# Inverse rows of the last task loaded step by step, 46 rows a load instead of 48, and three pairs of banks for the held groups

## What is computed

```python
# layer 0                                      # layer 1
f  = fft2(x);  Xh = (f.real - f.imag)[:, :, :46]   xf = rfft2(x)                      # complex
o1 = relu(Xh @ w1[0] + b1[0])                      o1r, o1i = relu(complex product with w1, + b1)
o2 = o1 @ w2[0] + b2[0]                            o2r, o2i = softshrink(complex product with w2, + b2)
x  = ifft2(softshrink(o2)).real + x                x = irfft2(o2r + 1j*o2i) + x
```

## Time and profile before

| what | us |
|---|---|
| runs, median (low to high) | 519.73 (518.99 to 520.14) |
| the profiled execution, its own time | 518.5 |
| its span, first to last instruction | 516.7 |
| PE busy | 475.7 (92%) |
| DVE, ACT, POOL busy | 306.7, 209.5, 173.1 |
| bytes read from and written to HBM | 52.21 and 51.43 MB |

### The profile page before, as it was taken

The page is one execution under the profiler, slowest core; times in us unless marked ns, Lnnn a source line. Parts: engine busy times, 40 slices in busy tenths (PEclk is TensorE's granted clock), DMA queues, the critical chain, the costliest instruction groups (busy, mean ns, idle before and its releaser), DMA issues.

```text
span 516.7 us, 14864 instructions
## 1 busy us (share of the span) xinstructions
PE 475.7 (92%) x6144; PEld 341.0 (66%) x6144; DVE 306.7 (59%) x674; ACT 209.5 (41%) x473; POOL 173.1 (34%) x194
## 2 busy tenths in 40 slices
PE   3479999999999999999999999999999999998773
PEld 1157787767777677767777776767777777876531
DVE  6534455457754677457754677456764577567643
ACT  0025544643445443543354442554355433434201
POOL 9822313223341344223441244313442123222124
PEclk9859999999999999999999999999999999999967
DMA  8889763667989588977889688977989565644397
GB/s 182 264 229 258 198 192 91 148 204 193 261 230 238 158 229 245 231 207 186 256 238 219 173 198 256 234 201 182 261 222 256 158 176 158 145 100 129 114 257 226
DMA packets 76864, 104.63 MB, mean 203 GB/s; under 512 B 7777, under 2 KB 63319, under 8 KB 76798
## 3 DMA queue, kind: packets, MB, share of 16 engines
q1 hardware_dynamic: 57766, 56.74, 41.1%
q0 software_dynamic: 10608, 40.45, 29.5%
q10 hardware_dynamic: 8424, 6.49, 5.1%
HBM read 52.21 MB, written 51.43 MB: 201 GB/s over the span
## 4 chain that ended last, share of the span: by engine, by line
PE 79%; DVE 6%; DMA 6%; POOL 3%; ACT 2%; issue 2%; SPq 1%; ACTq 1%; POOLq 0%; DVEq 0%
PE ps L620 14%; PE ps L686 13%; PE ps L711 12%; PE ps L673 11%; PE ps L587 10%; PE ps L633 8%; PE ps L698 5%; PE ps L649 4%; PE ps L659 3%; DMA img<-x 2%; DVE img L566 2%; DVE ns L540 2%; POOL xs L384 2%; ACT p L457 1%; DVE nt L518 1%
## 5 line engine op out<-in xcount | busy, mean ns | idle before, releaser
L566 DVE TENSOR_TENSOR img<-ps,img 90x768 f32<-90x768 f32 x92 | 82.6, 900 | 20.3 <-PE ps L620 16.9
L384 POOL TENSOR_TENSOR xs<-xs,nt 128x360 f32<-128x360 f32 (+1 forms) x48 | 41.6, 866 | 147.9 <-DVE nt L518 120.6
L620 PE MATMUL ps<-jr,cst 64*90 64x384 f32 (+1 forms) x358 | 81.5, 525 | 6.7 <-DVE img L566 5.7
L587 PE MATMUL ps<-img,cst 128*64 128x384 f32 (+1 forms) x368 | 70.8, 500 | 9.7 <-DMA img<-x 9.7
L393 POOL DMA_DIRECT2D y<-img x42 | 34.8, 828 | 133.5 <-DVE img L566 133.2
L450 ACT ACTIVATE o<-ps,wt 97x180 f32<-97x180 f32 (+1 forms) x96 | 33.8, 406 | 107.6 <-PE ps L673 107.6
L633 PEld LDWEIGHTS ps<-cst,bt 128*64 128x64 f32 x1472 | 63.2, 141 | 20.4 <-issue 13.9
L540 DVE SCALAR_TENSOR_TENSOR ns<-p,ps 109x384 f32<-109x384 f32 x96 | 53.2, 554 | 37.8 <-ACT p L457 32.9
L633 PE MATMUL ps<-cst,bt 128*64 128x90 f32 x1472 | 69.0, 248 | 6.1 <-DMA bt<-scr_f 6.1
L686 PE MATMUL ps<-wt,o 128*64 128x96 f32 x1472 | 73.9, 249 | 0.2 <-DVE o L532 0.2
L686 PEld LDWEIGHTS ps<-wt,o 128*64 128x64 f32 x1472 | 64.9, 137 | 12.3 <-issue 12.3
(11 more groups left out here) (41 smaller groups left out, 403.0 us busy)
## 6 DMA issues: line engine op xcount, KB each, us to landing
y<-img POOLq DMA_DIRECT2D x35, 540.0 KB, 5.4
img<-x POOLq DMA_DIRECT2D x30, 540.0 KB, 8.3
scr_i<-et SPq DMA_DIRECT2D x48, 270.0 KB, 5.6
scr_f<-fs SPq DMA_DIRECT2D x154, 72.0 KB, 3.3
bt<-scr_f SPq DMA_DIRECT2D x40, 270.0 KB, 5.2
jr<-scr_i SPq DMA_DIRECT2D x48, 216.0 KB, 5.3
img<-x ACTq DMA_DIRECT2D x10, 540.0 KB, 6.9
y<-img SPq DMA_DIRECT2D x11, 270.0 KB, 3.5
```

The source lines that it names most:

```text
L384: nc.gpsimd.tensor_tensor(re, re, nt[s % 2][:, :, 0:kws(s), 0:H], ALU.subtract).then_inc(re_ok, 1)
L566: nc.vector.tensor_tensor(y, p, y, ALU.add).then_inc(i_add, 1)
L587: last = mm(ps[64 * r:64 * r + 64, P3 + g % 2, 0:(b - a) * HC], K["w_fwd"], img[t % IMGS][:, a:b, :].rearrange("p h c -> p (h c)"), start= ...
L620: last = mm(ps[0:W, B0 + r, 0:n], K["w_inv"][64 * r:64 * r + 64, :], set_rows(t, j)[64 * r:64 * r + 64, at, 0:n], start=True, stop=True)
```

## The change

Three things are edited. The loads and stores of `scr_i` take only the 23 frequencies in use (`kws(s)` of a step, `2 * KW` = 46 rows) instead of 24. The last task's inverse rows go to `f0` (the first task's buffer, long free), eight rows with each step, behind the next step's store, and the last six behind the last store, half from SyncE and half from ScalarE; `jr` and `bt` aren't used for them. The held groups rotate over the bank pairs P2, P1, P3; and three groups, not four, go through ScalarE and GpSimd, over two buffers (`p1` and an idle `et`), and are stored from ScalarE's queue.

```diff
+HELD = 7
-LAST_POOL = (1, 4, 7, 10)
+LAST_POOL = (1, 4, 7)
...
     order += held
-    order += [("rows", TASKS - 1, j) for j in range(len(JSETS))]
+    order.append(("last_rows",))
     order += [("inv", TASKS - 1, g) for g in range(GROUPS)]
...
+        def last_rows(i, r):
+            k0, k1 = 2 * STEP * i, min(2 * STEP * (i + 1), 2 * KW)
+            rows = scr_i[TASKS - 1].rearrange("k e h c -> (k e) h c")[k0:k1]
+            four = rows[:, 0:H - 1, :].rearrange("q (g r s) c -> q g r (s c)", r=2, s=2)[:, :, r, :]
+            return four, f0[64 * r + k0:64 * r + k1, 0:GROUPS - 1, :], rows[:, H - 1, :], f0[k0:k1, GROUPS - 1, 0:HC]
+        def held_no(t, g):
+            return g - HELD if t == TASKS - 2 else -1
+        def pair_of(t, g):
+            if t == TASKS - 1:
+                return (P0, P1, P2, P3)[g % 4]
+            return (P2, P1, P3)[held_no(t, g) % 3] if held_no(t, g) >= 0 else P3
...
 # SyncE, a step's store
-                    sp.dma_start(scr_i[t][STEP * i:STEP * i + STEP].rearrange("k e h c -> (e h) k c"),
-                                 et[s % 2][0:2 * H, :, :]).then_inc(e_st[s % 2], 16)
+                    sp.dma_start(scr_i[t][STEP * i:STEP * i + kws(s)].rearrange("k e h c -> (e h) k c"),
+                                 et[s % 2][0:2 * H, 0:kws(s), :]).then_inc(e_st[s % 2], 16)
+                    if t == TASKS - 1 and i > 0:
+                        sp.wait_ge(e_st[(s - 1) % 2], 16 * ((s - 1) // 2 + 1))
+                        for r in range(2):
+                            four, to, one, to_one = last_rows(i - 1, r)
+                            sp.dma_start(to, four).then_inc(l_ld[0], 16)
+                        sp.dma_start(to_one, one).then_inc(l_ld[0], 16)
...
 # SyncE, a set of inverse rows (all tasks but the last)
-                    rows = scr_i[t].rearrange("k e h c -> (k e) h c")
+                    rows = scr_i[t].rearrange("k e h c -> (k e) h c")[0:2 * KW]
                     if g0 == GROUPS - 1:
-                        sp.dma_start(set_rows(t, j)[0:2 * KWP, 0, 0:HC], rows[:, 4 * g0, :]).then_inc(landed, 16)
+                        sp.dma_start(jr[k][0:2 * KW, 0, 0:HC], rows[:, 4 * g0, :]).then_inc(j_ld[k], 16)
...
-                            sp.dma_start(set_rows(t, j)[64 * r:64 * r + 2 * KWP, 0:g1 - g0, :], four[:, :, r, :]).then_inc(landed, 16)
+                            sp.dma_start(jr[k][64 * r:64 * r + 2 * KW, 0:g1 - g0, :], four[:, :, r, :]).then_inc(j_ld[k], 16)
+                if kind == "last_rows":
+                    sp.wait_ge(e_st[(NT - 1) % 2], 16 * ((NT - 1) // 2 + 1))
+                    four, to, one, to_one = last_rows(STEPS - 1, 0)
+                    sp.dma_start(to, four).then_inc(l_ld[0], 16)
+                    sp.dma_start(to_one, one).then_inc(l_ld[0], 16)
...
 # ScalarE, the three groups for GpSimd
-                    nc.scalar.activation(p1[0:W], ps[0:W, B0:B0 + 2, 0:2 * HC], ACT.Copy).then_inc(i_act, 1)
+                    if n > 1:
+                        act.wait_ge(i_pool, n - 1)
+                    p = (p1[0:W], et[NT % 2][0:W].rearrange("p (r s) c -> p r (s c)", r=2))[n % 2]
+                    nc.scalar.activation(p, ps[0:W, B0:B0 + 2, 0:2 * HC], ACT.Copy).then_inc(i_act, 1)
...
 # TensorE, inverse groups
+                        if n == 0:
+                            pe.wait_ge(d1_ss, 2 * NT)
+                        elif n == 1:
+                            pe.wait_ge(d0_ss, 2 * NT)
+                            pe.wait_ge(t_add, 2 * NT)
+                        elif n >= 3:
+                            pe.wait_ge(i_add, t * GROUPS + g - 2)
```

More of the change, by code:

```diff
@@ L220, in spectral_layers @@
         j_ld = [sem(f"j{k}_loaded") for k in range(JR)]
-        j_tail = [sem(f"last_set{j}_loaded") for j in range(JR, len(JSETS))]
+        l_ld = [sem(f"last_rows{k}_loaded") for k in range(2)]
+        y_last_act = sem("y_of_last_task_stored_act")
         i_mm, i_add = sem("inv_product"), sem("inv_added")
@@ L322, in _ @@
                     k, used = bank_of(t, j)
-                    landed = j_tail[j - JR] if t == TASKS - 1 and j >= JR else j_ld[k]
                     if j == 0:
@@ L328, in _ @@
                         sp.wait_ge(j_clr, j + 1)
-                    if t == TASKS - 1 and j >= JR:
-                        sp.wait_ge(a_mm, 2 * NT)
-                    elif used:
+                    else:
                         m = t * len(JSETS) + j - JR
@@ L340, in _ @@
                         for r in range(2):
-                            sp.dma_start(set_rows(t, j)[64 * r:64 * r + 2 * KWP, 0:g1 - g0, :], four[:, :, r, :]).then_inc(landed, 16)
-                if kind == "inv" and what[0] == TASKS - 1:
+                            sp.dma_start(jr[k][64 * r:64 * r + 2 * KW, 0:g1 - g0, :], four[:, :, r, :]).then_inc(j_ld[k], 16)
[4 more added lines that the diff above has]
+                    sp.dma_start(to_one, one).then_inc(l_ld[0], 16)
+                if kind == "inv" and what[0] == TASKS - 1 and what[1] not in LAST_POOL:
                     g, (h0, h1), (b, f) = what[1], hrows(what[1]), divmod(TASKS - 1, HALVES)
@@ L558, in _ @@
                     h0, h1 = hrows(g)
[L559 removed]
+                    B0 = pair_of(t, g)
                     dve.wait_ge(i_mm, t * GROUPS + g + 1)
@@ L616, in _ @@
                             pe.wait_ge(*last_added(g - 4))
+                    else:
+                        j = jset[g]
+                        k, _ = bank_of(t, j)
+                        if g == JSETS[j][0]:
+                            pe.wait_ge(j_ld[k], rows_landed(t, j))
+                        if n == 0:
[5 more added lines that the diff above has]
+                            pe.wait_ge(i_add, t * GROUPS + g - 2)
+                        else:
+                            vacate(0)
+                            vacate(1)
+                    rows, live = (f0[:, g, :], 2 * KW) if t == TASKS - 1 else (jr[k][:, g - JSETS[j][0], :], 64)
                     h0, h1 = hrows(g)
@@ L619, in _ @@
                         n = min(2, h1 - h0 - 2 * r) * HC
-                        last = mm(ps[0:W, B0 + r, 0:n], K["w_inv"][64 * r:64 * r + 64, :], set_rows(t, j)[64 * r:64 * r + 64, at, 0:n], start=True, stop=True)
+                        last = mm(ps[0:W, B0 + r, 0:n], K["w_inv"][64 * r:64 * r + live, :], rows[64 * r:64 * r + live, 0:n], start=True, stop=True)
                     last.then_inc(i_mm, 1)
```

51 lines of the change are left out of this document (23 added, 28 removed).

## The result

The changed kernel takes **670.98 us**, the median of four runs (666.34 to 674.06), and the kernel before 519.93 us on the same chip (518.99 to 521.73). The ratio is 1.290, with an interval of 1.2855 to 1.294. The profiled execution took 671.45 us with a span of 669.6 us; before, the span was 516.7, so 152.9 us are to be found.

What follows compares the result with a forecast made beforehand. TensorE was taken to set the pace, with transfers hidden but little room. From 518.5 us, 136 (six stalls), 19 (seventh), 21 (clock) and 12 (sets 3 and 4), less 5 (tail), gave 701.5, or 702 against the median; range 620 to 770.

Steps and rivals of the forecast that it cites:

- Two engines: Inverse loads: 46 rows go over two engines, always the same two, which need 25.7 to 36.0 us for six loads.
- The first reading: Splitting a load: every engine gets equally many rows, on the largest divisor up to 16; two engines for 46 rows.
- Rival A: Inverse loads stay spread, or their two engines change, so only the tail counts: 514.5 us (509 to 518), chance 0.15.
- 66 ns a piece: Inverse loads on two engines: assumed time of one 1536-byte piece, between 62 and 87 ns; 27.3 us for 414.
- ScalarE works in order, so TensorE soon stands too ... none of it hidden: Six tasks: late `fs` stores block ScalarE's copies, then TensorE, 22.6 us each, 136 us in all.
- Clock: TensorE after each pause: six microseconds at half speed lose 3 us, seven times, 21 us (7 to 35).
- Sets 3 and 4: Later inverse loads, mostly covered; GpSimd's waits for y stores add 2 us in six tasks, 12 us (0 to 30).
- Seventh time: Task 7: the `bt` load of step 46 stands behind the inverse loads; 19 us after 3.4 us of cover.
- The tail: After the last store: earlier last rows and a shorter series of copies and adds, 5 us off (2 to 8).
- I leave its 10.8 us: Tail: the last task's products keep their present length, half of it at the lower clock.
- B: Two engines, but only their work counts because TensorE goes on: 633 us (620 to 655), chance 0.12.
- C: Two engines, late y stores and refills cost every task another 10 us: 762 us (735 to 800), chance 0.13.

Runs made afterwards that it cites:

- e2: The changed kernel, still 46 rows, with each inverse load cut into one of 30 and one of 16 rows; 523.38 us, ratio 1.0091.
- e4: e1 with the last task's inverse products multiplying 64 rows instead of 46; 518.85 us, ratio 0.9989.
- e7: The kernel before, with the last task's inverse products multiplying 46 rows instead of 64, nothing else; 521.61 us, ratio 1.0042.
- e1: The changed kernel with 48-row loads of `jr` and full stores of four frequencies again, its tail still changed; 521.23 us, ratio 1.0046.
- e6: e4 with three y stores of task 6 held back until the last task's last rows have landed; 523.48 us, ratio 1.0079.
- e13: e4 with the eight rows of the step before the last issued ahead of the last store instead of behind it; 521.55 us, ratio 1.0046.
- e10: e4 with the last task's rows loaded as 16 at the third step, 16 at the fifth and 14 behind the last store; 518.3 us, ratio 0.9982.
- e12: e10 with three y stores of the task before the last held until the last rows have landed; 522.6 us, ratio 1.007.

## Why the prediction was right, and where not

Predicted were 702 us and slower; 671 came out. The direction, the edit that does it and the mechanism were right. The sum of 701.5 is 30 us above the profiled execution's 671.45: 40 too much for the seven tasks' stalls, 10 too little for the tail, so two errors partly cancel in it.

**Two engines: right.** The first reading (largest divisor up to 16) is shown by two small packets a load, by 49 GB/s on a DMA share of 0.13, and by e2, in which the same rows went over 15 and 16 engines (31 small packets) and the holes vanished. Rival A is excluded: the loads use the same engines each time, since their delays add up. The section of the Trainium skill that the prediction named, "Why a DMA increments its semaphore by 16 and not by 1" in "DMA: Bandwidth & Descriptors", gives this rule, and the trace agrees for 46, 90 and 48 rows.

**66 ns a piece: 62.7 measured**, the lower end. 414 pieces at 62.7 ns are 26.0 us, less 4.7 is 21.3 where 22.6 was forecast; ScalarE's waits are 21.6 on average, with the shorter ones of before in them.

**"ScalarE works in order, so TensorE soon stands too ... none of it hidden": only in part.** ScalarE around the pause:

```profile
265.29 0.47 ACT L454 ACTIVATE xs<-ps 128x360 f32<-128x360 f32 x1
287.22 0.87 ACT L445 ACTIVATE fs<-ps 112x384 f32<-112x384 f32 x2 [21.46 <-DMA scr_f<-fs]
```

It stops at 265.76; TensorE goes on to 269.19 and starts again 1.0 us after ScalarE. So 3.4 us are covered and 1.0 comes on top: of ScalarE's 21.46 TensorE sees 19.06. In six tasks the stall is 115 us, not 136.

**Clock: 3 us a time predicted, about 2.0 measured** (TensorE's busy time of a task against that of before). The clock was back about 4 us after the pause; I had taken six from the tail. **Sets 3 and 4: 2 us predicted, at most the 0.4 that is left over measured.** GpSimd's wait for y rose from 21.9 to 30.9 us in all, and next to none of it reached TensorE. Six tasks: 136 + 18 + 12 = 166 predicted, 130.1 measured.

**Seventh time: 19 + 3 = 22 predicted, 17.9 measured.** TensorE waited 16.1 us for `bt`, the place that the prediction gave.

**The tail, -5 predicted, +4.9 measured: the step that failed.** Two of its sentences were wrong. "I leave its 10.8 us": the last products took 15.02, because the change also cuts their rows from 64 to 46, and with 46 the clock does not come back (e4 and e7 show it, each by this edit alone; it costs 2.4 and 2.9 us of the medians). I had not costed that edit at all. And "six rows are a small part of it, so the last rows land" at 495.0: in e4 the first product came at 497.90, no earlier than 497.78 before. In the changed kernel the store before them also took 5.3 us to land where I reckoned with 2.6, and the first product came 7.7 after the rows' issue. In e1 and e4, with no 46-row loads left, it is still 8.0 and 6.6 us from the rows' issue to the first product. The eight-row loads, which I priced at 0 because the store that they wait for is a step old, are still moving when the six rows are issued (e6), and ahead of the store they delay it (e13). That they set the six rows' time isn't shown: e10 to e12 have none of them there, and their products begin 6.1 to 6.4 us after the issue. So why the last rows come late stays open. Even with the 64 rows back (e4) the tail is only 0.5 us shorter than before, 27.8 against 28.3, where 5 were forecast. The rest of the tail did what was said: the held groups run with two short gaps, and the copies and adds are no longer at the end.

**Rivals B and C.** B (only the engines' work counts, 633) falls to the 115.3 us in which TensorE waits for ScalarE. C (the overload feeds on itself, 762) would need tasks 10 us longer than the 87 of the forecast; they take 76.7 to 81.5, and the pauses, 18.1 to 20.1 us in the six tasks, don't grow from one to the next.

**Two loose readings.** From 509 us on one copy and two adds of the series are left, not all four. And 92 + 23 pieces at 66 ns are 7.6 us, or 6.8 with the 23, which are half as long, at half the price, not some 6. Neither changes the sum.

## What to carry to other kernels

Before trimming a transfer to the rows in use, look at how its rows divide: here 48 rows with two that hold nothing went over 16 engines, 46 over two, and in six tasks that cost 130 us for 4% fewer bytes in these loads. The count of small packets of one transfer in the DMA view told the number of engines: 2, 15 and 16 for 46, 90 and 48 rows. A transfer on few engines is paid for by whoever has a part on them behind it, here a store on the same queue, a copy that waits for its buffer, and TensorE behind that copy. And where a wait is to be shortened by loading most of the data earlier, first measure what the last small piece takes by itself: here the first product came 6.0 (e6) to 8.0 us (e1) after the six rows were issued, while the loads of a first set of 48 rows landed 4.6 to 5.3 us after theirs.

## What the runs showed that I had not expected

- Products over 46 rows kept TensorE at 0.50 of its clock for 15 us of unbroken work, where products over 64 rows in the same place had it at 1.00 after some 3 to 6 us (e1 against e4, the kernel before against e7).
- Packets of the short loads behind the last store took 127 ns (e6) and 187 ns (e12) on average with nothing of y in flight, against 66 ns by the same working in the long loads on two engines. The cause is open.
- Issuing slows with the transfers: the six loads took SyncE 16.94 us to issue where they took 2.79.
